# A third bank pair for spread queries and one bank for message sums, in the attention of a two-layer graph transformer

## What is computed

```python
for l in range(2):
    xn = layernorm(h); q, k, v = heads(xn @ wq), heads(xn @ wk), heads(xn @ wv)   # 8 heads of 32
    scores = einsum('ehd,ehd->eh', q[dst], k[src]) * scale
    m = segment_max(scores, dst); ex = exp(scores - m[dst]); z = segment_sum(ex, dst)
    agg = segment_sum((ex / z[dst])[:, :, None] * v[src], dst)
    h = h + agg @ wo + bo
    h = h + gelu(layernorm(h) @ w1 + b1) @ w2 + b2
```

## Time and profile before

| | us |
|---|---|
| median of three runs | 5863.71 (5830.56 to 5882.23) |
| profiled execution | 5855.11, its span 5853.4 |
| TensorE matmuls busy | 4279.6 (73%) |
| VectorE (DVE) | 3776.8 (65%) |
| POOL | 3331.1 (57%) |
| ScalarE (ACT) | 2449.6 (42%) |
| TensorE's mean granted clock | 0.871 |
| first and last product (line 875) start | 458.5 and 4716.1 |

### The profile page before, as it was taken

The page is one execution under the profiler, slowest core; times in us unless marked ns, Lnnn a source line. Parts: engine busy times, 40 slices in busy tenths (PEclk is TensorE's granted clock), DMA queues, the critical chain, the costliest instruction groups (busy, mean ns, idle before and its releaser), DMA issues. The chain is left out here.

```text
span 5853.4 us, 97652 instructions
## 1 busy us (share of the span) xinstructions
PE 4279.6 (73%) x19304; PEld 3223.2 (55%) x19305; DVE 3776.8 (65%) x11017; ACT 2449.6 (42%) x6871; POOL 3331.1 (57%) x3037
## 2 busy tenths in 40 slices
PE   0696787777777777777596777777777777777678
PEld 0344555555555557667444555555555556676645
DVE  3695777777777755445386777777777754444456
ACT  0114566555555533333113555555555533333211
POOL 1215555555555548888714555555555538888844
PEclk9897888888889888888797898888888888888879
DMA  8336666666666646666535666666666646666656
GB/s 205 108 120 185 184 194 194 187 193 190 191 189 194 171 108 125 132 127 122 98 115 177 181 192 187 186 181 190 193 188 191 185 110 129 131 118 130 114 152 170
DMA packets 644706, 942.13 MB, mean 161 GB/s; under 512 B 121917, under 2 KB 468685, under 8 KB 644525
## 3 DMA queue, kind: packets, MB, share of 16 engines
q0 software_dynamic: 263808, 538.03, 38.9%
q1 hardware_dynamic: 350317, 375.73, 20.7%
q10 hardware_dynamic: 30528, 27.80, 1.6%
HBM read 810.39 MB, written 130.86 MB: 161 GB/s over the span
## 5 line engine op out<-in xcount | busy, mean ns | idle before, releaser
L747 POOL DMA_INDIRECT kv<-kv_scratch,src_u x1792 | 1749.1, 976 | 1450.1 <-DVE msg L890 1011.3
L1009 PE MATMUL sum_p<-msg,hot_s 128*128 128x273 f32 x3584 | 1183.7, 458 | 575.0 <-ACT msg L803 226.5
L1211 POOL DMA_INDIRECT sum_scratch<-ysum,dest x800 | 1261.2, 1576 | 245.4 <-issue 165.9
L1009 PEld LDWEIGHTS sum_p<-msg,hot_s 128*128 128x128 f32 x3584 | 699.2, 215 | 870.9 <-issue 575.4
L998 PE MATMUL qe<-queries,hot_q 128*128 x3584 | 1089.1, 432 | 90.8 <-issue 60.4
L875 DVE TENSOR_TENSOR prod<-qe,kv 128x512 f32<-128x512 f32 x896 | 612.9, 684 | 484.6 <-issue 289.9
L998 PEld LDWEIGHTS qe<-queries,hot_q 128*128 128x128 f32 x3584 | 752.5, 215 | 295.4 <-issue 134.5
L764 ACT ACTIVATE S<-qe 128x16 f32<-128x16 f32 x896 | 172.4, 192 | 1114.7 <-PE qe L998 526.2
L882 DVE TENSOR_REDUCE S<-prod 128x16 f32<-128x512 f32 x896 | 609.8, 681 | 4.8 <-DVE prod L875 0.2
L890 DVE TENSOR_TENSOR msg<-kv,W 128x512 f32<-128x512 f32 x896 | 610.9, 682 | 2.4 <-ACT W L835 1.9
L787 ACT ACTIVATE far<-iota_f,ndrel_u 128x128 f32<-128x128 f32 x1792 | 572.3, 390 | 3.0 <-issue 0.2
(11 more groups left out here) (228 smaller groups left out, 5946.9 us busy)
## 6 DMA issues: line engine op xcount, KB each, us to landing
drow<-drel_scratch SPq DMA_DIRECT2D x224, 512.0 KB
ea<-in_edge_attr SPq DMA_DIRECT2D x100, 512.0 KB
srow<-in_src_rows SPq DMA_DIRECT2D x100, 512.0 KB
kv<-kv_scratch,src_u POOLq DMA_INDIRECT x1792
kv_scratch<-res SPq DMA_DIRECT2D x100, 256.0 KB, 2.0
hin<-h_scratch SPq DMA_DIRECT2D x154, 128.0 KB
h_scratch<-res SPq DMA_DIRECT2D x150, 128.0 KB, 1.7
masks<-mask_scratch SPq DMA_DIRECT2D x112, 128.2 KB
```

The source lines that it names most:

```text
L747: g.indirect_dma_start(out=kv[:, slot, :], out_offset=None, in_=KVd, in_offset=bass.IndirectOffsetOnAxis(ap=src_u[:, par, u:u + 1], axis=0 ...
L1009: ins = pe.matmul(sum_p[g % 2][:, 0:XW], hot_s[:, (j // 2) % 2, (2 * j + u) % 4, :], msg[:, g % 2, u, :], start=(u == 0), stop=(u == 1))
L1211: g.indirect_dma_start(out=sum_d[r], out_offset=bass.IndirectOffsetOnAxis(ap=dest[:, k, j:j + 1], axis=0), in_=ysum[:, k, j, :], in_offset ...
```

## The change

- `qe` gets a third buffer of two banks. Which buffer a pair of a period uses stands in `QE`, how many pairs back the buffer was last used in `QE_BACK`.
- `spread` runs two pairs ahead (`AHEAD`); pairs 0 and 1 of the next period are spread in steps 6 and 7. The tile numbers are read one place further on (`PE_AT`).
- `sum_p` is one bank; `sum_up` waits for the addition just before it.
- `small` is gone. Its row ends, edge columns and scale products stand in the second half of the bank `turned`.
- The matmul for `scale` moves behind the two transposes that turn the exponentials back and shares their semaphore `wT_s`; `delta_s` is gone.
- ScalarE copies own scores ahead of the weights of the message.

```diff
-PE_AT = GB - 1
+PE_AT = GB - 2
+AHEAD = 2
+QE = (0, 1, 2, 0, 1, 2, 0, 1)
+QE_BACK = (2, 2, 5, 3, 3, 3, 3, 3)
...
-                qe = [ph.enter_context(nc.psum_tensor(f"qe{j}_{l}", [P, 2, 512], f32)) for j in range(2)]
-                sum_p = [pb(ph, f"sum_p{j}") for j in range(2)]
+                qe = [ph.enter_context(nc.psum_tensor(f"qe{j}_{l}", [P, 2, 512], f32)) for j in range(3)]
+                sum_p = pb(ph, "sum_p")
                 turned = pb(ph, "turned")
-                small = pb(ph, "small")
...
                         def period(n, par, t):
                             for g in range(GB):
+                                if g + 1 < GB and has_scores(n):
+                                    own_scores(n, par, g + 1)
+                                if g + 1 == GB and has_scores(n + 1):
+                                    own_scores(n + 1, 1 - par, 0)
                                 mj = message(n, g)
...
-                                if g + 1 < GB and has_scores(n):
-                                    own_scores(n, par, g + 1)
-                                if g + 1 == GB and has_scores(n + 1):
-                                    own_scores(n + 1, 1 - par, 0)
...
                                 if g == 3 and has_chain(n):
-                                    a.wait_ge(delta_s, n)
+                                    a.wait_ge(wT_s, n)
                                     wait(a, rescaled, n * 2 - 2)
-                                    a.activation(scale[:, :], small[:, 2 * P + H:2 * P + 2 * H], ACT.Exp).then_inc(scale_s, 1)
-                                    a.wait_ge(wT_s, n)
+                                    a.activation(scale[:, :], turned[:, 2 * P + H:2 * P + 2 * H], ACT.Exp).then_inc(scale_s, 1)
...
                             pe.wait_ge(hot_q_s, n * 4 + q + 1)
-                            wait(pe, prod_s, c - 1)
+                            wait(pe, prod_s, c - QE_BACK[g] + 1)
                             for u in range(2):
-                                ins = pe.matmul(qe[g % 2][:, u, 0:QW], hot_q[:, q % 2, (2 * g + u) % 4, :],
+                                ins = pe.matmul(qe[QE[g]][:, u, 0:QW], hot_q[:, q % 2, (2 * g + u) % 4, :],
...
-                            wait(pe, add_s, c - 1)
+                            wait(pe, add_s, c)
                             pe.wait_ge(msg_s, c + 1)
                             for u in range(2):
-                                ins = pe.matmul(sum_p[g % 2][:, 0:XW], hot_s[:, (j // 2) % 2, (2 * j + u) % 4, :],
+                                ins = pe.matmul(sum_p[:, 0:XW], hot_s[:, (j // 2) % 2, (2 * j + u) % 4, :],
...
-                                if g + 1 < GB and has_scores(n):
-                                    spread(n, par, g + 1, tiles[g])
-                                if g + 1 == GB and has_scores(n + 1):
-                                    spread(n + 1, 1 - par, 0, tiles[g])
+                                if g + AHEAD < GB and has_scores(n):
+                                    spread(n, par, g + AHEAD, tiles[g])
+                                if g + AHEAD >= GB and has_scores(n + 1):
+                                    spread(n + 1, 1 - par, g + AHEAD - GB, tiles[g])
...
-                                        pe.matmul(small[:, 2 * P + H:2 * P + 2 * H], chain[0:1, 2 * P:3 * P], delta[0:1, :],
-                                                  start=True, stop=True).then_inc(delta_s, 1)
...
-                                    pe.transpose(turned[:, P:2 * P], ex[:, 1, :], ident[:, :]).then_inc(wT_s, 1)
+                                    pe.transpose(turned[:, P:2 * P], ex[:, 1, :], ident[:, :])
+                                    pe.matmul(turned[:, 2 * P + H:2 * P + 2 * H], chain[0:1, 2 * P:3 * P], delta[0:1, :],
+                                              start=True, stop=True).then_inc(wT_s, 1)
```

More of the change, by code:

```diff
@@ L664, in attend @@
                 scT_s, shift_s, chain_s, ends_s, cols_s = s.many(5)
-                exp_s, wT_s, w_s, delta_s, scale_s, rescaled = s.many(6)
+                exp_s, wT_s, w_s, scale_s, rescaled = s.many(5)
                 CK = 11
@@ L874, in products @@
                             wait(v, red_s, n * GB + g)
-                            v.tensor_tensor(out=prod[:, :, :], in0=qe[g % 2][:, :, 0:D],
+                            v.tensor_tensor(out=prod[:, :, :], in0=qe[QE[g]][:, :, 0:D],
                                             in1=kv[:, par * UB + 2 * g:par * UB + 2 * g + 2, 0:D],
@@ L899, in add @@
                             at = sums[:, bass.ds(tile * XW, XW)]
-                            v.tensor_tensor(out=at, in0=at, in1=sum_p[g][:, 0:XW], op=ALU.add).then_inc(add_s, 1)
+                            v.tensor_tensor(out=at, in0=at, in1=sum_p[:, 0:XW], op=ALU.add).then_inc(add_s, 1)
                         def step(i, k):
@@ L922, in chain_rows @@
                             v.wait_ge(chain_in, n * 16)
-                            v.tensor_tensor_scan(left[0:1, par, 1:P + 1], chain[0:1, 0:P], small[0:1, 0:P], -BIG,
+                            v.tensor_tensor_scan(left[0:1, par, 1:P + 1], chain[0:1, 0:P], turned[0:1, 2 * P:3 * P], -BIG,
                                                  ALU.add, ALU.max).then_inc(chain_s, 1)
                             v.tensor_tensor_scan(right[0:1, 0:P][:, ::-1], chain[0:1, P:2 * P][:, ::-1],
-                                                 small[0:1, P:2 * P][:, ::-1], -BIG, ALU.add, ALU.max).then_inc(chain_s, 1)
+                                                 turned[0:1, 3 * P:4 * P][:, ::-1], -BIG, ALU.add, ALU.max).then_inc(chain_s, 1)
                             v.wait_ge(chain_s, step(n, 3))
@@ L937, in chain_edges @@
                             v.wait_ge(cols_s, n)
-                            v.tensor_tensor(out=begin[:, :], in0=small[:, 2 * P:2 * P + 3], in1=not_first[:, :],
+                            v.tensor_tensor(out=begin[:, :], in0=turned[:, 2 * P:2 * P + 3], in1=not_first[:, :],
                                             op=ALU.add).then_inc(chain_s, 1)
@@ L971, in period @@
                                         v.wait_ge(rescaled, n * 2)
-                                    add(lo + g, (g - 1) % 2, tiles[g])
+                                    add(lo + g, tiles[g])
                                 if has_chain(n):
@@ L1034, in period @@
                                         wait(pe, scale_s, n - 1)
-                                        pe.transpose(small[0:1, 0:P], run_l[:, P - 1:P], ident[:, :])
-                                        pe.transpose(small[0:1, P:2 * P], run_r[:, 0:1], ident[:, :]).then_inc(ends_s, 1)
+                                        pe.transpose(turned[0:1, 2 * P:3 * P], run_l[:, P - 1:P], ident[:, :])
+                                        pe.transpose(turned[0:1, 3 * P:4 * P], run_r[:, 0:1], ident[:, :]).then_inc(ends_s, 1)
                                     elif g == 2:
@@ L1040, in period @@
                                                                  left[0:1, 1 - par, UB:UB + P])):
-                                            ins = pe.matmul(small[:, 2 * P + i:2 * P + i + 1], row, ones[0:1, 0:1],
+                                            ins = pe.matmul(turned[:, 2 * P + i:2 * P + i + 1], row, ones[0:1, 0:1],
                                                             start=True, stop=True)
@@ L1064, in period @@
                                     pe.transpose(turned[:, 0:P], ex[:, 0, :], ident[:, :])
-                                    pe.transpose(turned[:, P:2 * P], ex[:, 1, :], ident[:, :]).then_inc(wT_s, 1)
+                                    pe.transpose(turned[:, P:2 * P], ex[:, 1, :], ident[:, :])
+                                    pe.matmul(turned[:, 2 * P + H:2 * P + 2 * H], chain[0:1, 2 * P:3 * P], delta[0:1, :],
+                                              start=True, stop=True).then_inc(wT_s, 1)
                         pe.wait_ge(consts, 1)
                         pe.wait_ge(dve_ready, 4)
-                        first, = registers(PE_E, nt_pe[0:1, PE_AT:PE_AT + 1])
-                        spread(0, 0, 0, first)
+                        first = registers(PE_E, nt_pe[0:1, PE_AT:PE_AT + AHEAD])
+                        for g in range(AHEAD):
+                            spread(0, 0, g, first[g])
                         periods(pe, period, 0, LAST_N)
```

4 lines of the change are left out of this document (2 added, 2 removed).

## The result

The changed kernel takes 6038.26 us (median of four runs, 6034.53 to 6039.79), the kernel before, in runs beside it, 5872.97 us (5830.56 to 5890.8). The ratio is 1.029, 95% interval 1.023 to 1.035: slower by 165 us. The profiled execution has a span of 6037.3 us against 5853.4.

What follows compares the result with a forecast made beforehand. No engine was full; VectorE idled 7.1 of 28.2 us a period, mostly for late-told TensorE completions. Idle terms 6.1 + 0.6 + 0.75 + 0.6 = 8.05 us gave +0.95 a period, 5855 + 105 = 5960 us, range 5650 to 6080.

Steps and rivals of the forecast that it cites:

- The stall moves from the products to the additions: At the period seam, VectorE's 4.1 us wait before L875 goes; 6.1 us a period stands before L900; chance 0.50.
- the late stretch catches the sum of step 6: Rival: VectorE stops at step 7's addition, runs stay at eight gathers; -0.25 us a period, 5828 or 5762 us; chance 0.14.
- the late stretch: Part of each period's seam where TensorE's completions are told late; one computed result was told 4.6 us late.
- Its cause as told, POOL's gathers on end: At the seam, after some 5 us of uninterrupted gathers TensorE's completions are told late, all through only when POOL has stopped.
- That the moved spread moves the stall: Spreading the next period's pair 0 in step 6, not 7, frees the products, moving the stall 1.8 us of VectorE work later.
- The chain's waits: VectorE's waits before row scans (L923), 0.40 to 0.6 us a period, and before the rescaling (L980), 0.45 to 0.75.
- elsewhere: VectorE's remaining idle time in a period: some 0.4 us before, plus 0.2 us for the chain's edges, 0.6 us.
- The one bank, "nothing in general": Message sums waiting for the addition before them are covered by the next product, message and scores; 0.8 us a period at most.
- Stall independent of POOL: Rival: the seam stall's end stays put and 1.8 us of work hides in it; -1.45 us a period, 5695 us; chance 0.16.
- nothing to tell: Rival: gathers, TensorE and late completions together hold the period at 28.2 us however waits are dealt out; 5855 us; chance 0.15.
- 1.95: VectorE's idle us a period besides the stall: 0.6 at L923, 0.75 at L980 and 0.6 elsewhere.
- The sign: Whole kernel: the change makes it slower, by +0.95 us a period, 105 us; chance of slower 0.42.

## Why the prediction was right, and where it was not

**The stall moves from the products to the additions: right, and larger than forecast.** Forecast 6.1 us a period before L900, measured 6.04 before L901; products forecast at nothing, measured 0.17; runs of ten gathers in nearly every seam. That 6.04 meets 6.1 so closely is partly luck. By place in the step, in the middle periods of the two layers, the addition of the sum of step 7 waits 5.2 and 5.9 us, and the one before it, for the sum of step 6, 0.8 and 0.6. That is the rival "the late stretch catches the sum of step 6" come true in part, yet the runs stay at ten gathers. And the late stretch reaches the maximum too (below). The Trainium skill's rule that a gap which repeats can mean too few buffers (Perfetto Trace Analysis, Optimization Strategy) would have said otherwise: with a third buffer the gap left the products, as it says, but VectorE's idle time a period did not fall, 7.1 us before and 8.7 after (1300 less 920.65 us, over 43.5 periods). The time came out 78 us over the forecast and inside the range.

**Its cause as told, POOL's gathers on end: wrong as a sufficient cause.** Gathers are needed (5132 us without them against 6057). But runs of sixteen and thirty-two pass without lateness on prompt chips. All three seams of the earlier trace rows came from one chip, and the onset after some 5 us of gathers held for that chip. That all is told only when POOL has stopped does not hold either: in the seam above the addition at 1512.19 comes while two more gathers are still to be issued. What about a late chip holds completions back stays open: the bytes, POOL's issuing and the path of the events were not separated there, because no later run fell on such a chip. Nor can a trace whose matmul ends are modelled tell a matmul that is done and told late from one that ran late. That three in ten records are missing in just those traces would fit a path of events that is full; but records of VectorE and ScalarE are missing in about the same share, and theirs on record are all on time. The Trainium skill (NOTIFIC — the notification-queue block, Overflow: three behaviours, one of which stalls the engine) says that a queue of records that is full can drop records or stall the engine that makes them. Missing records are in these traces; no run here shows that a queue was full or that recording holds an engine.

**That the moved spread moves the stall: not shown.** With one bank alone the stall stood before the additions too, on the other late chip.

**The chain's waits, forecast +0.5 us a period over before (L923 0.2, L980 0.3): right for one, wrong for the other, and a term left out.** Row scans 0.69 against 0.6 forecast, rescaling 0.39 against 0.75. The step that failed is the sum of VectorE's idle time: its 0.6 "elsewhere" is the 0.4 of before and 0.2 for the edges, and the 0.56 before the maximum (L910), which the prediction lists itself, stands in no term. Measured after the change are 0.87 on the late chip. Forecast and measured in the window of 600 to 1900 us, 8.05 and 8.7 us, differ by that 0.87, 0.17 at the products, 0.09 at the scans, minus 0.06 at the additions, minus 0.36 at the rescaling and next to nothing elsewhere.

This wait is two different things. On the late chip 34.0 of its 37.9 us are 11 of 43 waits of over 1 us, as at 1516.41 above, and 24.2 of 25.7 us were 6 of 46 before the change: pieces of the late stretch. On the prompt chip 42 of 44 wait, each 0.4 to 0.9 us; there it rises from 0.05 to 0.61 us a period. I had followed the moved spreads to VectorE and not to what stands behind them in TensorE's own queue in step 0, where the turned scores now come behind the spread of pair 2. Putting them ahead removed the wait, on two prompt chips; on a late one it wasn't tried. How much of it belongs to the one bank and how much to a one-hot matrix that comes late was not separated.

**The one bank, "nothing in general": wrong at the ends of the layers.** My cover was the next product, message and scores. Behind the last product of a layer there is no product or scores, so sum and addition take turns. With one bank alone that makes the ends 29.6 us long, about 6 us a layer more, at full clock. In the changed kernel they are 36 to 38 us, 12 to 15 a layer more, because the clock falls to 0.50 as well. Which other part of the change brings the half clock is open; the spreads two ahead are not it, since with spreads one ahead it falls too. The ends are 25 us of the 184 on the late chip and 29 of 89 on the prompt one. I had multiplied a period's sum by 110 and not looked at the periods that are not like the others.

The gap of 79 us between the forecast 105 and the 184 of the traces is then 25 us at the ends, 4 outside the attention, and 49 between the first and last products, where 154 us came (88.0 and 66.4) and 105 were forecast.

**The rivals.** "Stall independent of POOL" (5695) and "nothing to tell" are out for the chip of the result; "sum of step 6 caught" came in part, without its runs of eight and its gain. Its 5762 us should have been 5756, since a third of 1.95 is 0.65 us a period. On a prompt chip none of my cases would have held: no stall to move, and +78 us from the ends of the layers and waits that I had costed at 0.5 us a period or nothing. The sign was the same there, for another reason than the one I gave.

## What to carry to other kernels

Cost an edit in the first and last turns of a loop too: a wait that is covered by other work in the steady state is bare where that work has run out, and the clock can fall with it (0.50 in the changed kernel's ends, 1.00 with one bank alone). When work moves ahead in a queue, list what stands behind its new place. And a stall whose releasers are missing from the trace is to be seen on a second chip before a mechanism is built on it; here a stage took 28 us a period on one chip and 22 on another with the same program.

## What was not expected of the hardware

The kernel before took 5135 to 6069 us over five chips; the runs on one chip lie within 0.5% of each other, and within 1.0% on the chip of the result. In the attention stage the mean granted clock was 0.88 on the late chip and 1.00 on the prompt one, where TensorE does not stand at each seam. On the late chips 26 to 33 of 100 semaphore updates have no record with full gathers, on the prompt ones at most 1 in 100. Late are TensorE's updates alone, by up to 7.7 us. A gather lasts 1018 ns on the prompt chip and 979 on the late one, so POOL's own speed is not what differs. Left without its stalls, the kernel before has two engines nearly full: VectorE is busy 948.5 of 1000 us, and on POOL 724 gathers take 736.7 and the gaps between those on end 187.1 more, 924 in all. The group by line, 600 to 1600 us:

```profile
L747 POOL DMA_INDIRECT kv<-kv_scratch,src_u x724 | 736.7, 1018 | 265.0 <-issue 187.1 <-DVE msg L890 77.9
```
